# A gated mixer with routed experts: splits, transposes, combines and router work moved to other steps

## The reference

```python
xn = layernorm(x)                              # per token, over 128 channels
# mixer: xx = previous token - token; lin = (xn + xx * mix) @ W.T for r, w, k, v, a, g
u = sigmoid(lin_a) * tanh(lin_k) * lin_v
state = state * exp(-softplus(lin_w)) + u      # scan over the 256 tokens
mixed = sigmoid(lin_r) * state                 # then normalized in 16 groups of 8 channels
s = (groupnorm(mixed) * gn_w + gn_b) * sigmoid(lin_g) @ W_out.T + b_out
# experts, 4 rounds on cur = xn, 4 experts of width 512, the best 2 per token:
cur = cur + sum_e cw[:, e] * (gelu(cur @ W1[e] + b1[e]) @ W2[e] + b2[e])
out = x + s * silu(cur)
```

## Time and profile before

| | before |
|---|---|
| three runs | 821.64, 823.02, 823.14 us, median 823.02 |
| the profiled execution | 823.14 us, span 821.3 us from first to last instruction |
| PE busy | 803.9 us, 98% of the span |
| DVE busy | 714.8 us, 87% |
| ACT busy | 652.2 us, 79% |
| POOL busy | 115.0 us, 14% |
| mean granted TensorE clock | 0.993 |
| largest groups | L382 gelu, 512 of 681 ns; L619 g_lo, 256 of 1221 ns; L386 g_hi, 256 of 1062 ns |

### The profile page before, as it was taken

The page is one execution under the profiler, slowest core; times in us unless marked ns, Lnnn a source line. Parts: engine busy times, 40 slices in busy tenths (PEclk is TensorE's granted clock), DMA queues, the critical chain, the costliest instruction groups (busy, mean ns, idle before and its releaser), DMA issues. The chain is left out here.

```text
span 821.3 us, 10635 instructions
## 1 busy us (share of the span) xinstructions
PE 803.9 (98%) x3656; PEld 651.3 (79%) x3656; DVE 714.8 (87%) x1339; ACT 652.2 (79%) x911; POOL 115.0 (14%) x135
## 2 busy tenths in 40 slices
PE   8899999999999999999999999999999999899996
PEld 7787788888788887888888887888878888678885
DVE  6978888889997979988898898898989898889897
ACT  7798887887887877888788886888778887678874
POOL 0010211111111111111111101111111111011110
PEclk9999999999999999999999999999999999999998
DMA  9333463342533415423164422644226343174532
GB/s 255 116 78 91 102 162 84 96 97 39 143 59 83 97 33 142 103 49 94 29 152 100 95 39 39 142 103 104 39 54 164 93 116 72 19 180 115 129 65 51
DMA packets 44468, 78.50 MB, mean 96 GB/s; under 512 B 6656, under 2 KB 23552, under 8 KB 40448
## 3 DMA queue, kind: packets, MB, share of 16 engines
q0 software_dynamic: 18144, 33.04, 23.9%
q1 hardware_dynamic: 25136, 44.64, 16.5%
q10 hardware_dynamic: 1136, 0.16, 0.1%
HBM read 40.34 MB, written 2.36 MB: 52 GB/s over the span
## 5 line engine op out<-in xcount | busy, mean ns | idle before, releaser
L382 ACT ACTIVATE g<-h_bank,b_c 128x512 f32<-128x512 f32 x512 | 329.3, 681 | 80.2 <-PE h_bank L853 78.5
L619 DVE TENSOR_TENSOR g_lo<-g,g_hi 128x1024 fp32r<-128x1024 f32 x256 | 307.9, 1221 | 73.6 <-ACT g_hi L386 72.6
L386 ACT ACTIVATE g_hi<-g 128x1024 fp32r<-128x1024 f32 x256 | 271.7, 1062 | 8.1
L322 POOL DMA_DIRECT2D cur<-tmp x126 | 113.9, 904 | 692.1 <-DVE tmp L633 572.4
L849 PE MATMUL h_bank<-cur_hi,w_hi 128*128 128x512 f32 x512 | 206.3, 403 | 1.2 <-ACT g L382 0.7
L909 PE MATMUL y_bank<-g_hi,w_hi 128*128 128x512 f32 x512 | 203.4, 397 | 2.8 <-issue 2.2
L853 PE MATMUL h_bank<-cur_lo,w_hi 128*128 128x512 f32 x512 | 204.1, 399 | 0.0
L850 PE MATMUL h_bank<-cur_hi,w_lo 128*128 128x512 f32 x512 | 203.1, 397 | 0.0
L910 PE MATMUL y_bank<-g_hi,w_lo 128*128 128x512 f32 x512 | 203.0, 397 | 0.0
L914 PE MATMUL y_bank<-g_lo,w_hi 128*128 128x512 f32 x512 | 140.9, 396 | 2.2 <-DVE g_lo L619 2.2
L909 PEld LDWEIGHTS y_bank<-g_hi,w_hi 128*128 128x128 f32 x512 | 96.5, 188 | 26.5 <-issue 2.6
(11 more groups left out here) (120 smaller groups left out, 516.9 us busy)
## 6 DMA issues: line engine op xcount, KB each, us to landing
cur<-tmp POOLq DMA_DIRECT2D x126, 256.0 KB, 3.4
cw_b<-cw_scratch SPq DMA_DIRECT2D x31, 1024.0 KB, 5.1
cur<-in_x SPq DMA_DIRECT2D x8, 256.0 KB, 5.5
xn_t<-cur SPq DMA_DIRECT2D x8, 256.0 KB, 2.8
xr<-in_x SPq DMA_DIRECT2D x8, 256.0 KB, 3.2
out<-o SPq DMA_DIRECT2D x7, 256.0 KB, 2.4
cw_b<-in_w SPq DMA_DIRECT2D x4, 256.0 KB, 5.2
cw_b<-cw_scratch SPq DMA_DIRECT2D x1, 768.0 KB, 5.2
```

Of the source, the lines that this page charges most:

```text
L322: pool.dma_start(cur[:, block_of(s // E)], tmp[:, s % 2, :], accum_op=ALU.add).then_inc(summed, DMA)
L382: nc.scalar.activation(g[:, gb, ft * BLK:(ft + 1) * BLK], hb[ft][:, :], ACT.Gelu_apprx_tanh, bias=b1_c[:, e * FT + ft:e * FT + ft + 1]).th ...
L386: nc.scalar.activation(g_hi[:, gb, h], g[:, gb, h], ACT.Copy).then_inc(g_hi_done, 1)
L619: nc.vector.tensor_tensor(g_lo[:, gb, h], g[:, gb, h], as_f32(g_hi[:, gb, h]), ALU.subtract).then_inc(g_lo_done, 1)
```

## The change

The warm-up has 40 transposes instead of 52, and the four FILL transposes go. Blocks 2 to 7 are scaled and turned one step later, and split one step later. Splits of blocks 4 to 7 move on DVE from ahead of `g_low_half` to behind it, where those of 2 and 3 are. `logits(1)` stays in step 6, `logits(2)` moves from 12 to 13. Statistics and spread of blocks 2 and 3 move from step 1, ahead of the combines, to step 2; the root follows in step 3; for blocks 4 to 7 the statistics of two move from step 3 to 4 and the spread from 6 to 5. `router_scores(2)` moves from step 13 to 14; `router_gates(1)` and `(2)` move from the head of steps 8 and 14 to between the g_low halves of steps 8 and 15. Step 16 joins LATE. In the end phase DVE runs the mixer stage first, then `end_output`, then `end_scaled` and `end_product`; `end_output` was behind `g_low_half`. PE runs `turn_product(b)` at the end of step 102 + 4b, not in step 103 + 4b between up and down.

```diff
--- before.py
+++ after.py
@@ -20,7 +20,7 @@
 LN_EPS = 1e-5
 GN_EPS = 0.00064
 RSQRT_SEED = float(0x5F3759DF)
-WARM_UP, FILL = 52, 4
+WARM_UP = 40
 DMA = 16
 SPLITS = 5
 QUADS = 4
@@ -46,13 +46,13 @@
 
 
 NORM_GROUPS = [(0, 1), (2, 3), (4, 5, 6, 7)]
-NORM_SCALE = {2: 3, 3: 4, 4: 7, 5: 8, 6: 9, 7: 10}
-SPLIT_AT = {2: 4, 3: 5, 4: 8, 5: 9, 6: 10, 7: 11}
+NORM_SCALE = {2: 4, 3: 5, 4: 8, 5: 9, 6: 10, 7: 11}
+SPLIT_AT = {2: 5, 3: 6, 4: 9, 5: 10, 6: 11, 7: 12}
 SPLIT_AT.update({8: 25, 9: 25, 10: 27, 11: 27})
 SPLIT_AT.update({k: 4 * (k - 4) + (1 if k % 2 == 0 else -1) for k in range(12, TURNS)})
-LOGITS_AT = {0: 0, 1: 6, 2: 12}
+LOGITS_AT = {0: 0, 1: 6, 2: 13}
 LOGITS_AT.update({n: 16 * n - 20 for n in range(3, len(BATCHES))})
-LATE = (0, 8)
+LATE = (0, 8, 16)
 
 
 def mixers_at(s):
@@ -198,10 +198,10 @@
 
         r_jobs = {}
         for s in range(STEPS):
-            if s > END_FROM and (s - END_FROM) % E == 3:
-                r_jobs["end", (s - END_FROM) // E] = len(r_jobs)
             for n in at_step(LOGITS_AT, s):
                 r_jobs["logits", n] = len(r_jobs)
+            if s >= END_FROM + 2 and (s - END_FROM - 2) % E == 0:
+                r_jobs["end", (s - END_FROM - 2) // E] = len(r_jobs)
 
         def block_of(k):
             return slice(k % NB * BLK, (k % NB + 1) * BLK)
@@ -447,7 +447,7 @@
                     router_tanh(1)
                 elif s == 13:
                     high_mixw()
-                elif s == 14:
+                elif s == 15:
                     router_tanh(2)
                 for m, stage in mixers_at(s):
                     if stage in TAKES:
@@ -766,29 +766,21 @@
             for s in range(STEPS):
 
                 if s == 2:
+                    norm_stats(NORM_GROUPS[1])
+                    norm_spread(NORM_GROUPS[1])
+                elif s == 3:
                     norm_root(NORM_GROUPS[1])
-                elif s == 3:
+                elif s == 4:
                     norm_stats(NORM_GROUPS[2][0:2])
                 elif s == 5:
                     norm_stats(NORM_GROUPS[2][2:4])
+                    norm_spread(NORM_GROUPS[2])
                 elif s == 6:
-                    norm_spread(NORM_GROUPS[2])
                     norm_root(NORM_GROUPS[2])
-                elif s == 7:
-                    router_scores(1)
-                elif s == 8:
-                    router_gates(1)
-                elif s == 13:
-                    router_scores(2)
                 elif s == 14:
-                    router_gates(2)
                     low_mixw()
-                for k in at_step(SPLIT_AT, s):
-                    if NB // 2 <= k < NB:
-                        split_cur(k)
-                if s > END_FROM and (s - END_FROM) % E == 2:
-                    end_scaled((s - END_FROM) // E)
-                    end_product((s - END_FROM) // E)
+                if s - 1 in (6, 13):
+                    router_scores({6: 1, 13: 2}[s - 1])
                 for m, stage in mixers_at(s):
                     if stage == 0:
                         mixer_input(m, 0, (P_R, P_W))
@@ -802,6 +794,11 @@
                         mixer_norm(m)
                     elif stage == 6:
                         mixer_gate(m)
+                if s > END_FROM and (s - END_FROM) % E == 3:
+                    end_output((s - END_FROM) // E)
+                if s > END_FROM and (s - END_FROM) % E == 2:
+                    end_scaled((s - END_FROM) // E)
+                    end_product((s - END_FROM) // E)
                 for k in at_step(SPLIT_AT, s):
                     if k >= NB:
                         split_cur(k)
@@ -809,20 +806,15 @@
                 for half in range(2):
                     if s + 1 < STEPS:
                         g_low_half(s + 1, half)
-                    if half == 0 and s == 0:
-                        router_gates(0)
+                    if half == 0 and s in (0, 8, 15):
+                        router_gates({0: 0, 8: 1, 15: 2}[s])
 
                 if s == 0:
                     low_w2(2)
                     low_w2(3)
-                elif s == 1:
-                    norm_stats(NORM_GROUPS[1])
-                    norm_spread(NORM_GROUPS[1])
                 for k in at_step(SPLIT_AT, s):
-                    if k < NB // 2:
+                    if k < NB:
                         split_cur(k)
-                if s > END_FROM and (s - END_FROM) % E == 3:
-                    end_output((s - END_FROM) // E)
                 for n in at_step(LOGITS_AT, s - 1):
                     if n >= 3:
                         router_scores(n)
@@ -951,8 +943,6 @@
             for _ in range(WARM_UP):
                 nc.tensor.transpose(rb[:, 0:D], ident[:, :], ident[:, :])
             turn_normed(0)
-            for _ in range(FILL):
-                nc.tensor.transpose(rb[:, 0:D], ident[:, :], ident[:, :])
             up(0)
             turn_normed(1)
 
@@ -961,8 +951,6 @@
                     up(s + 1)
                 if s == 0:
                     logits(0)
-                if s > END_FROM and (s - END_FROM) % E == 3:
-                    turn_product((s - END_FROM) // E)
                 down(s)
                 for b in at_step(NORM_SCALE, s):
                     turn_normed(b)
@@ -982,6 +970,8 @@
                         turn_mixer(m, J_MN, mn, mn_ready)
                     elif stage == 6:
                         project_out(m)
+                if s > END_FROM and (s - END_FROM) % E == 2:
+                    turn_product((s - END_FROM) // E)
 
             pe.wait_ge(z_ready, NB)
             for t in range(TPB):
```

## The result

The changed kernel takes 842.04 us (median of four runs, 840.96 to 843.23; two more took 842.36, the profiled one, and 845.06); the kernel before took 823.08 us in the runs beside it. The ratio is 1.0239, with a 95% interval of 1.0211 to 1.0266. The forecast was 841.6 us, 2.2% slower.

The account below looks back on a forecast made before the run. PE, busy 803.9 of 821.3 us, was taken as the bound, so anything making it wait lengthens the run. The terms summed to +18.5 us on 823.1, giving 841.6 us, 2.2% slower, range 832 to 848 us.

Parts of the forecast that it names:

- step 1: Ahead of down(2): the stall for combine(0) and the slow matmuls behind it go, -3.6 us.
- step 2: Inside logits(1): PE waits for block 3's split, now queued behind both g_low halves, +4.3 us (bounds 0.8 and 5.3).
- step 3: Transposes of blocks 5 to 7 wait for DVE's copy, +3.5 then +3.0 us each; the combine(8) wait goes, -0.9.
- step 4: Behind the four new waits at logits(1) and the transposes: low clock costs 1.6 us each, +6.4 us (bounds 0 and 8.8).
- Step 5: Opening: with fewer warm-up transposes PE idles longer and the clock may fall in up(0), +0.6 us (bounds 0 and 1.6).
- step 6: End phase: PE waits for z at loop step 110, net +3.1 us; waits at 106 and 114 go, -0.9.
- Rival A: Stalls come, but the clock mostly stays up or DVE is less behind: 833 us, chance 14%.
- B: Faster: the copy out of p_bank is done before PE needs it: 821.4 or 818.3 us, chance 6%.
- C: Stalls feed on each other: longer low clock, late gates for combine(8), a stall at logits(2): 850 us, chance 12%.
- D: No change: gains at down(2) and combine(8) balance only the stall at 110 and half a logits wait; chance 2%.

Follow-up runs that it names:

- run 9: Kernel before, with only statistics and spread of blocks 2 and 3 moved to the head of loop step 2, ahead of their root: 821.24 us, ratio 0.9971.
- 1: Changed kernel, with the splits of blocks 4 to 7 ahead of both g_low halves again, tables kept: 829.15 us, ratio 1.0070.
- run 2: Kernel before, with only the splits of blocks 4 to 7 moved behind both g_low halves of their loop step: 837.95 us, ratio 1.0168.
- run 3: Changed kernel, with 26 identity transposes put ahead of each of the three waiting transposes to keep PE busy: 839.3 us, ratio 1.0203.
- run 6: Changed kernel, with the end phase of the kernel before (DVE's end work and turn_product in their old places): 840.29 us, ratio 1.0208.
- run 7: Changed kernel, with 52 instead of 40 warm-up transposes, FILL still out: 842.84 us, ratio 1.0228.
- 5: Changed kernel, with logits(1) in loop step 7 and router_scores(1) at the head of loop step 8: 841.1 us, ratio 1.0219.
- 4: Changed kernel, with blocks 2 and 3 scaled, turned and split in the loop steps of the kernel before: 843.71 us, ratio 1.0244.
- run 10: Kernel before, with statistics and spread of blocks 2 and 3, combine(8), DVE's end work and turn_product re-placed: 818.84 us, ratio 0.9935.

## Why the prediction was right

By its own steps, from the two traces. Each is the length of a stretch after, less that before, or a new wait's own length.

| step | forecast | measured | where |
|---|---|---|---|
| 1, gap ahead of down(2) and the clock | -3.6 | -3.4 | up(3) to up(4), 9.53 to 6.17 |
| 2, wait inside logits(1) | +4.3 | +4.6 | logits to up(8), 0.94 to 5.58, two of its matmuls slow |
| 3, first wait for the copy | +3.5 | +3.5 | 83.92 to 87.39 |
| 3, second and third | +6.0 | +5.5 | 2.71 + 2.81 |
| 3, combine(8) no longer waited for | -0.9 | -0.9 | up to down(10), 3.65 before |
| 4, four slow ups | +6.4 | +5.9 | 3.83, then 4.43 three times, less 2.80 |
| 5, the opening | +0.6 | +1.6 | up(3) at 30.39 against 28.82 |
| 6, step 110 | +3.1 | +3.3 | end of down(110) to down(112), 13.34 to 16.60 |
| 6, steps 106 and 114 | -0.9 | -1.0 | 7.03 to 6.76 and 7.50 to 6.76 |
| sum | +18.5 | +19.1 | spans differ by 19.3 |

The two lengths for steps 106 and 114 are from the end of one down to the end of the next.

Steps 1 and 3 are shown by the traces and by runs that do or undo them alone (9, and 1 and 2); step 4 for the three later waits by run 3, in its profile. For step 6, run 6 shows the places of the waits, and the profiles of all runs the sign, but no run shows its 2.3 us alone. The table also says which edits were free, as far as one trace shows it: behind the scores and gates a step later, LATE at 16 and the later turn of blocks 4 to 7, PE has no wait. They were not run alone.

Some points were less right than the sum. Step 5 was mis-sized: 1.6 us in this execution, of which 0.3 us is up(0) starting later (12.56 against 12.25) and the rest its low clock; and it was put down to the removed transposes, where run 7 and run 2 show the low clock with 52 transposes too, and runs 3 and 5 a high one with 40: it changes from execution to execution. The middle of the bounds was a fair guess for the median, not a reason. Step 2 has the right wait, but runs 4 and 5 show that its opposite is not worth 4.6 us: with the root of blocks 2 and 3 or the scores at their neighbouring places, ACT loses as much. I read step 2 as a mistake of one table entry; it is a region in which DVE and ACT have no slack, and in the two placements tried the wait went to the next user. The bounds of steps 3 and 4 were set as if independent; run 3 shows that a clock that stays up makes the later waits 3.5 us each. The lower bound of step 2, 0.8 us, leaves out the 1.15 us of the split itself. And two readings of the rows were wrong without changing the sum: the largest idle time of the kernel before is not 2.15 us but the 3.41 us ahead of the last block's transposes, and the later warm-up transposes start 0.09 us apart, not 0.12.

Rival A needed a clock that stays up. In the changed kernel's own trace it did not. It did behind the first wait in run 7 (up(11) took 2.9 us), and the next wait was then 3.30 us of idle with an up of 5.2 behind it, so the sum stayed; and behind the third wait of runs 2 and 5. Rivals B, C and D had no sign in the trace of the changed kernel.

## What to carry to other kernels

Price a move within an in-order queue by what the instruction now stands behind is itself waiting for, not by its length: the copy takes 0.68 us, DVE was idle for 2.54 us ahead of it, and PE paid 3.5. Where three engines pass one tile around in a ring, a wait of one is not made up by the others' slack, since they stand still for it too. And before taking a wait out, ask what is late next at every neighbour: a wait of 4 us went to another place twice here (runs 4 and 5). The 2.15 us one disappeared where the statistics were put into idle time of DVE (run 10), or cost 1.0 us elsewhere where they ran in the same step as the root that uses them (run 9).

## What the runs showed of the hardware

Identity transposes alone held the clock (run 3): with 26 of them in each wait it stayed at 1.00, with some 0.5 us of idle left, where idle of 2.3 us and more was followed by the 1.2 GHz level in all cases but one (3.30 us in run 7). Below that either happened. 2.15 us was followed by it; the third waits of runs 2 and 5 (2.27 and 2.25 us) were not, and their ups took 2.9 us. The wait inside down(111), 1.83 to 1.85 us with 0.4 behind it, was followed by it in the kernel before and in run 9, and not in runs 2 and 6. A low stretch is not paid on top of a wait in full when the next wait depends on the same ring: 1.6 us lost in an up took 0.7 to 0.8 off the wait that followed (2.8 and 2.7 us, against 3.5 in run 3). And with one and the same opening of 40 transposes, the first up took 4.5 to 4.6 us in four executions and 3.1 in two.
